# Roots of the layer norms on GpSimd, and the row maxima of attention split after one transpose

## The reference

```python
x = x + _L0_xattn_ref(_layernorm(x), ctx, ...)   # 8 heads of 8 channels, 256 positions, rotary
x = x + _L0_ffn_ref(_layernorm(x), ...)          # 64 experts, top 8, width 96
x = x + _L1_xattn_ref(_layernorm(x), ctx, ...)
x = x + _L1_ffn_ref(_layernorm(x), ...)

def _layernorm(x, axis=-1, eps=1e-05):
    m = jnp.mean(x, axis=axis, keepdims=True)
    v = jnp.var(x, axis=axis, keepdims=True)
    return (x - m) / jnp.sqrt(v + eps)
# in attention, per head:
scores = jnp.einsum('bhtc,bhsc->bhts', q, k) / math.sqrt(K_CH)
p_attn = jax.nn.softmax(scores, axis=-1)
```

## Time and profile before

| | us |
|---|---|
| median of 3 runs | 2429.53 (2429.11 to 2438.61) |
| the profiled execution | 2436.11 |
| its span in the profile | 2434.3 |
| busy in it: PE, DVE, ACT, POOL | 1719.1, 1632.6, 1215.9, 963.7 |

### The profile page before, as it was taken

The page is one execution under the profiler, slowest core; times in us unless marked ns, Lnnn a source line. Parts: engine busy times, 40 slices in busy tenths (PEclk is TensorE's granted clock), DMA queues, the critical chain, the costliest instruction groups (busy, mean ns, idle before and its releaser), DMA issues. The chain is left out here.

```text
span 2434.3 us, 45523 instructions
## 1 busy us (share of the span) xinstructions
PE 1719.1 (71%) x12720; PEld 1137.5 (47%) x12879; DVE 1632.6 (67%) x5762; ACT 1215.9 (50%) x3109; POOL 963.7 (40%) x878
## 2 busy tenths in 40 slices
PE   1488888888883688888888347777777777755651
PEld 0244444444441577777777214344444344434431
DVE  3588888888883334444432368999999999983331
ACT  0266666666671345555555226656556556642120
POOL 0115555555556000000000255555655656227883
PEclk9899999999996799999999759999999999988896
DMA  6855656565546875445454577665666656408856
GB/s 154 192 141 166 170 165 169 168 170 170 166 140 203 277 227 159 154 152 161 152 158 151 192 186 200 165 167 157 159 168 158 167 152 161 120 28 223 184 98 109
DMA packets 420687, 399.24 MB, mean 164 GB/s; under 512 B 46171, under 2 KB 392667, under 8 KB 420443
## 3 DMA queue, kind: packets, MB, share of 16 engines
q1 hardware_dynamic: 345163, 264.16, 39.2%
q0 software_dynamic: 37904, 90.22, 14.6%
q10 hardware_dynamic: 37376, 41.96, 5.9%
HBM read 242.00 MB, written 178.42 MB: 173 GB/s over the span
## 5 line engine op out<-in xcount | busy, mean ns | idle before, releaser
L786 ACT ACTIVATE prob<-psE 128x512 f32<-128x512 f32 x1024 | 600.0, 600 | 389.6 <-PE psE L1378 377.5
L987 DVE TENSOR_REDUCE mx<-psS 128x2 f32<-128x512 f32 x1024 | 682.9, 676 | 93.8 <-PE psS L1367 81.5
L674 POOL DMA_INDIRECT yg<-y_d,posb x256 | 263.3, 1029 | 880.6 <-DVE posb L1047 593.5
L1378 PE MATMUL psE<-q,k 128*128 128x256 bf16 x2048 | 397.9, 277 | 44.1 <-DMA q<-mrow 17.9
L1316 DVE TENSOR_TENSOR hid<-sil,psE 128x96 f32<-128x96 f32 x384 | 97.6, 254 | 429.1 <-ACT sil L872 428.7
L1367 PE MATMUL psS<-k,q 128*128 128x512 bf16 x865 | 339.5, 395 | 51.6 <-DMA k<-k_stack_d 31.4
L1483 PE MATMUL psE<-wt,xgT 128*128 (+1 forms) x1536 | 330.8, 340 | 0.3
L662 POOL DMA_INDIRECT xs_d<-xr,posi x256 | 250.6, 979 | 187.6 <-ACT prob L786 146.4
L1477 PE MATMUL psS<-ident,xg 128*128 128x128 f32 x768 | 158.4, 289 | 194.4 <-DMA xg<-xn_d,idx 83.1
L867 ACT COPY xgT<-psS 128x256 f32<-128x256 f32 x384 | 144.4, 376 | 288.8 <-PE psS L1477 254.7
L1378 PEld LDWEIGHTS psE<-q,k 128*128 128x128 bf16 x2048 | 194.2, 99 | 185.1 <-ACT prob L786 26.0
(11 more groups left out here) (209 smaller groups left out, 2842.5 us busy)
## 6 DMA issues: line engine op xcount, KB each, us to landing
xg<-xs_d SPq DMA_DIRECT2D x320, 128.0 KB, 2.1
y_d<-y_all SPq DMA_DIRECT2D x320, 128.0 KB, 1.8
q<-q_stack_d SPq DMA_DIRECT2D x128, 256.0 KB
k<-k_stack_d SPq DMA_DIRECT2D x128, 256.0 KB
wt<-in_gu ACTq DMA_DIRECT2D x128, 192.0 KB, 3.8
wt<-in_dn ACTq DMA_DIRECT2D x128, 96.0 KB, 4.2
q_stack_d<-parts SPq DMA_DIRECT2D x64, 192.0 KB
k_stack_d<-parts SPq DMA_DIRECT2D x64, 192.0 KB
```

What stands on the lines that cost most here:

```text
L674: g.indirect_dma_start(yg[:, k, :], None, y0_d[:, :], bass.IndirectOffsetOnAxis(posb[b][:, k:k + 1], 0)).then_inc(d_yg, 16)
L786: a.activation(prob[gr][:, u % 4, :], psE[ring][:, :], ACT.Exp, scale=SCALE).then_inc(s_exp, 1)
L987: v_.tensor_reduce(mx[b][:, bg // 4, :].rearrange("p (h r) -> p h r", h=2)[:, :, (bg % 4) * 2 + tt], psS[(UNITS * (st.s0 - LAG["smax"]) + ...
L1378: ins = m_.matmul(psE[ring][:, i * T:(i + 1) * T], k2[b][:, bg, hh * T + i * P:hh * T + (i + 1) * P], q2[b][:, bg, :], start=True, stop=True)
```

## The change

1. **Roots.** POOL computes them at the head of the step, ahead of its first indirect DMA: two operations on 128x2 (variance plus epsilon, negated mean), a power of -0.5, and a product, with a wait between those that depend on each other. The twelve DVE instructions go. ACT waits for the new count in unit 6, and DVE waits for it in unit 15, before it overwrites `mv`.
2. **Maxima.** The reduction writes negated maxima (`negate=True`). PE transposes 16 columns of f32 directly (`mT1` as before in unit 1, `mT0` in unit 10 instead of 11). ACT copies the transpose as bf16 (`mhi`; half 0 in unit 11 instead of 12), and DVE subtracts that from the transpose (`mlo`; half 1 in unit 3, half 0 in unit 12). SP sends `mhi` and `mlo`, one DMA each, after `mlo`. The bank is free only after `mlo`. L995, L1003 and L1004 go.
3. In layer 1 DVE's residual (L1132) moves from unit 10 to unit 9 and the comparison L1143 from 9 to 10.

```diff
+    def roots(self):
+        return self.s0 - LAG["front"] + 1 + self.L * (STEPS - LAG["front"] - 2)
...
-        FREE = dict(mT0=s_mrow[0], mT1=s_mrow[1], V=s_v, OT0=s_nrm[0], OT1=s_nrm[1], Q=s_qr, K=s_kr,
+        FREE = dict(mT0=s_mlo[0], mT1=s_mlo[1], V=s_v, OT0=s_nrm[0], OT1=s_nrm[1], Q=s_qr, K=s_kr,
...
-                    hold(sp, s_mrow[1], st.n("attn"))
-                    for hh in range(2):
-                        sp.dma_start(q2[b][64 * hh + MAXROW:64 * hh + MAXROW + 2, 4:8, :].rearrange("p g t -> p (g t)"),
-                                     mrow[1][16 * hh:16 * hh + 16, :]).then_inc(d_max[1][b], 16)
+                    hold(sp, s_mlo[1], st.n("attn"))
+                    for i, part in enumerate((mhi[1], mlo[1])):
+                        sp.dma_start(q2[b][MAXROW + i:MAXROW + i + 65:64, 4:8, :].rearrange("p g t -> p (g t)"),
+                                     part[:, :]).then_inc(d_max[1][b], 16)
...
+            g.memset(power[:, :], -0.5)
...
+                if st.on("front") or st.on("route"):
+                    if st.on("front"):
+                        pool.wait_ge(s_mvx, st.n("front"))
+                    if st.on("route"):
+                        pool.wait_ge(s_mvr, st.n("route"))
+                    done = 4 * (st.roots() - 1)
+                    wait(pool, s_rstd, done)
+                    g.tensor_scalar(ve[:, :], mv[:, :, 1], EPS, None, ALU.add).then_inc(s_rstd, 1)
+                    g.tensor_scalar(below[:, :], mv[:, :, 0], -1.0, None, ALU.mult).then_inc(s_rstd, 1)
+                    pool.wait_ge(s_rstd, done + 2)
+                    g.tensor_tensor(rstd[:, 0, :], ve[:, :], power[:, :], ALU.pow).then_inc(s_rstd, 1)
+                    pool.wait_ge(s_rstd, done + 3)
+                    g.tensor_tensor(rstd[:, 1, :], below[:, :], rstd[:, 0, :], ALU.mult).then_inc(s_rstd, 1)
                 moved(0, PACE[0])
...
-                    a.copy(mrow[h][:, :], psM[item_bank(L, f"mT{h}")][0:32, 0:P]).then_inc(s_mrow[h], 1)
+                    a.copy(mhi[h][:, :], psM[item_bank(L, f"mT{h}")][0:16, 0:P]).then_inc(s_mhi[h], 1)
...
-                    if u == 12 and st.on("smax"):
+                    if u == 11 and st.on("smax"):
                         max_rows("smax", 0)
                     if u == 6 and (st.on("front") or st.on("route")):
-                        act.wait_ge(s_rstd, st.it * 3 + (st.s0 - 1 + L * (STEPS - 4)))
+                        act.wait_ge(s_rstd, 4 * st.roots())
...
-                                     psS[...][:, :].rearrange("p (h s) -> p h s", h=2), AX.X, ALU.max)\
+                                     psS[...][:, :].rearrange("p (h s) -> p h s", h=2), AX.X, ALU.max, negate=True)\
...
-                def negate_max(h):
-                    ...
-                def split_max(h):
-                    ...
+                def split_max(stage, h):
+                    dve.wait_ge(s_mhi[h], st.n(stage))
+                    v_.tensor_tensor(mlo[h][:, :], psM[item_bank(L, f"mT{h}")][0:16, 0:P], mhi[h][:, :], ALU.subtract)\
+                      .then_inc(s_mlo[h], 1)
...
-                    if u <= 5 and norms:
-                        newton(2 * u)
...
-                    if u < 5 and norms:
-                        newton(2 * u + 1)
...
+                    if u == 3 and st.on("attn"):
+                        split_max("attn", 1)
+                    if u == 12 and st.on("smax"):
+                        split_max("smax", 0)
...
+                    if u == 15 and (st.on("front") or st.on("route")):
+                        dve.wait_ge(s_rstd, 4 * st.roots())
...
-                        product("mT1", "attn", [(s_msp[1], st.n("attn", 2))],
-                                [(msp[1][:, :, :, :].rearrange("p h a r -> p (h a r)"), None)], s_mT[1])
+                        product("mT1", "attn", [(s_max, st.n("attn", UNITS))],
+                                [(mx[st.buf("attn")][:, 1, :], None)], s_mT[1])
...
-                    if u == 11 and st.on("smax"):
-                        product("mT0", "smax", [(s_msp[0], st.n("smax", 2))],
-                                [(msp[0][:, :, :, :].rearrange("p h a r -> p (h a r)"), None)], s_mT[0])
+                    if u == 10 and st.on("smax"):
+                        product("mT0", "smax", [(s_max, st.n("smax", UNITS, 8))],
+                                [(mx[st.buf("smax")][:, 0, :], None)], s_mT[0])
```

More of the change, by code:

```diff
@@ L49 @@
 EPS = 1e-5
-MAGIC = 1597463007.0
 STRIDE = TOKENS
@@ L187, in build @@
         tok0 = sb("tok0", [P, 1])
+        power = sb("power", [P, 2])
         part_i = sb("part_i", [P, 1], I32)
@@ L240, in build @@
         mx = [ab(f"mx{b}", [P, 2, 16]) for b in range(NB)]
-        mhi = [ab(f"mhi{h}", [P, 2, 8], BF16) for h in range(2)]
-        msp = [ab(f"msp{h}", [P, 2, 2, 8]) for h in range(2)]
-        mrow = [ab(f"mrow{h}", [32, P], BF16) for h in range(2)]
+        mhi = [ab(f"mhi{h}", [16, P], BF16) for h in range(2)]
+        mlo = [ab(f"mlo{h}", [16, P], BF16) for h in range(2)]
         v = [ab(f"v{b}", [P, 2, UNITS, 32]) for b in range(NB)]
@@ L251, in build @@
         stats = ab("stats", [P, 2, 6])
-        nwt = ab("nwt", [P, 6, 2])
+        ve = ab("ve", [P, 2])
+        below = ab("below", [P, 2])
         rstd = ab("rstd", [P, 2, 2])
@@ L590, in body @@
                     b = st.buf("smax")
[L591 to L594, removed]
+                    hold(sp, s_mlo[0], st.n("smax"))
+                    for i, part in enumerate((mhi[0], mlo[0])):
+                        sp.dma_start(q2[b][MAXROW + i:MAXROW + i + 65:64, 0:4, :].rearrange("p g t -> p (g t)"),
+                                     part[:, :]).then_inc(d_max[0][b], 16)
                 if st.on("back"):
@@ L770, in max_rows @@
                     act.wait_ge(s_mT[h], st.n(stage))
-                    wait(act, d_max[h][(st.s0 - LAG[stage] - 1) % NB], Step(L, st.s0 - 1, st.it).nbuf(stage, 32)
-                         if st.s0 - 1 >= LAG[stage] else 0)
-                    a.copy(mrow[h][:, :], psM[item_bank(L, f"mT{h}")][0:32, 0:P]).then_inc(s_mrow[h], 1)
+                    before = Step(L, st.s0 - 1, st.it)
+                    if before.s0 >= LAG[stage]:
+                        act.wait_ge(d_max[h][before.buf(stage)], before.nbuf(stage, 32))
+                    a.copy(mhi[h][:, :], psM[item_bank(L, f"mT{h}")][0:16, 0:P]).then_inc(s_mhi[h], 1)
                 for u in range(UNITS):
@@ L1114, in body @@
                         normalise(1)
-                    if u < 5 and norms:
-                        newton(2 * u + 1)
-                    if u == 5 and norms:
-                        ch.join("newton")
-                        v_.scalar_tensor_tensor(rstd[:, 1, :], mv[:, :, 0], -1.0, rstd[:, 0, :], ALU.mult, ALU.mult)\
-                          .then_inc(s_rstd, 1)
                     if L == 0 and u == 8 and st.on("front"):
@@ L1124, in body @@
                         rotate(1)
-                    if u == 8 and st.on("smax"):
-                        negate_max(0)
-                    if L == 1 and u == 10 and st.on("back"):
+                    if L == 1 and u == 9 and st.on("back"):
                         b = st.buf("back")
@@ L1137, in body @@
                         v_.tensor_reduce(posf[b][:, :], hot[:, :, :], AX.X, ALU.add).then_inc(s_posf, 1)
-                    if u == 8 and st.on("smax"):
-                        split_max(0)
-                    if u == 9 and st.on("place") and L == 1:
+                    if u == 10 and st.on("place") and L == 1:
                         b = st.buf("place")
@@ L1179, in body @@
                             v_.tensor_copy(topf[b][:, :], topi[b][:, :]).then_inc(s_topf, 1)
-                    if u == 15 and st.on("smax"):
-                        negate_max(1)
                     if u == 14 and st.on("back"):
@@ L1196, in body @@
                         v_.bn_aggr(mv[:, 1, :], stats[:, 1, :]).then_inc(s_mvr, 1)
-                    if u == 15 and st.on("smax"):
-                        split_max(1)
                     if u == 15 and st.on("comb"):
```

38 lines of the change are left out of this document (2 added, 36 removed).

## The result

The changed kernel takes 2450.1 us (median, 2443.3 to 2455.1) beside 2430.2 us (2428.7 to 2438.6) for the kernel before on the same chip. The ratio is 1.0065, with a 95% interval of 1.005 to 1.008: slower by 0.65%, where 3.4% faster was forecast. Later runs of the changed kernel on another chip gave 1.004 (1.0028 to 1.0053).

A forecast was written before the change was run, and what follows sets the result against it. DVE was taken to bound layer 1, with DVE, PE and POOL taking turns in layer 0. Savings of 25 us (layer 0) and 57 us (layer 1), 82 together, took 2429.5 to 2348 us; own range 2325 to 2370, cost bounds 2312 to 2394.

The forecast's parts named there:

- rival (e): POOL's power is long: past 7.2 us in layer 0 ACT waits in unit 6; 2457 us at 8.9 us; chance 5%.
- V's bank: PSUM bank for PE's V product, freed by the unit 3 subtraction: PE waits later for the rotation anyway, so no cost.
- the blocking 0.5 us a step: Layer 1, DVE waiting for POOL: 0.5 of the Newton steps' 1.5 us of waiting stays; bounds 0 and 1.5.
- Rival (a): Layer 1's additions inherit the waiting for POOL; layer 1 saves 0.9 us a step, 27 us; 2378 us; chance 17%.
- Layer 1's term of 1.9 us: DVE in layer 1: 2.76 less 0.4 less 0.5 us saved a step, 57 us over thirty steps; bounds 27 and 75.
- Layer 0: 0.85 forecast: DVE between mask and rotation in layer 0: 0.85 us saved a step, 25 us over thirty steps; bounds 9 and 42.
- The nearer bound: Layer 0's low bound: 0.3 us a step (9 us), if PE takes DVE's place in its third of the loop.
- DVE's wait for the logits: Sign expected in layer 0: DVE's wait for the router's logits, 0.92 us before, grows to about 2 us.
- SP's queue: Half 1's rows and the loads behind them go about four and a half us later in layer 1; fits, counted 0.
- rival (b): The loads come late: layer 1's step stays at 22, layer 0 gains nothing; 32 us saved, 2398 us; chance 13%.
- POOL's four operations: POOL's new work on 128x2 each step: 1.5 us for the four with waits, between 0.6 and 4.7, covered by existing waits.
- rival (d): Negation in DVE's reduction costs 0.08 us each for 1024 reductions, 82 us, cancelling the gain; 2430 us; chance 4%.

The follow-up runs named there:

- third run: Changed kernel with half 1's subtraction in DVE's unit 1 instead of 3, both layers; ratio 0.9805 to the kernel before.
- the eleventh: Changed kernel, subtraction still in unit 3, with POOL's L704 and L705 of layer 1 behind the second gather, not the first; ratio 0.9913.
- eighth run: Kernel before with only the maxima's part, DVE keeping Newton, half 1 subtracted in unit 3 in layer 0 and unit 1 in layer 1; ratio 1.0049.
- sixth run: Changed kernel with subtraction in unit 3 in layer 0 and 1 in layer 1, plus layer 1's L704 and L705 ahead of POOL's first gather; ratio 0.977.

## Why the prediction was wrong

It forecast 2348 us, and even rival (e), the slow side, needed a power of 8 us. Step by step:

**V's bank: the step that failed.** The prediction says: "V's bank now comes free with the subtraction in unit 3 and no longer with ACT's copy in unit 1; by the same starts PE would come to V some 0.2 us early, and it waits later in the loop for the rotation anyway, so nothing." That was worked out from the rows of layer 0, and there it held: V's product waits for `mlo` once in 400 us, 0.5 us. It was never asked for layer 1, which has no rotation, and where PE stands further ahead of DVE. The trace of the kernel before shows it: V's product starts 2.9 us before DVE is through with its third addition, behind which the subtraction was to go.

```profile
1654.89 0.61 PE L1409 MATMUL psM<-proj_v,ctx 128*128 128x128 f32 x4
1657.31 0.47 DVE L1084 SCALAR_TENSOR_TENSOR x<-yg,w_all,x 128x256 f32<-128x256 f32 x1
```

Layer 1 had a later wait to hide it in, Q's for `nrm`, but of 1.6 us only. The subtraction's place was worth 2 to 2.5 us a step there: 24.16 and 24.33 with unit 3, 21.84 and 22.08 with units 2 and 1. That figure holds both what the subtraction sets free, V's bank and SP's queue; that the bank alone is enough is shown by 24.44 us with the loads early. The wait was named, but not who is queued behind it (the scores of the next units), nor what DVE does in front of the subtraction in the other layer.

**What stands ahead of the subtraction.** The prediction gave the blocking 0.5 us a step (the addition takes 1.33 us over) and asked only how much DVE work it adds. Its place mattered more: 1.6 to 1.8 us of the loss are the blocked addition right ahead of the subtraction that PE waits for (unit 3 with POOL's pair later, 22.56). The two unseen costs do not simply add: unit 3 without the blocking costs 0.7 us, and the blocking behind the subtraction costs V nothing.

**Rival (a), the additions inherit the waiting,** had the mechanism: the third addition takes 1.80 us. Its size for the whole change was 0.9 us a step in layer 1. With the subtraction in unit 2 or 1, so with V's bank out of the way, the change gives 1.4 and 1.2; the roots alone give 0.95, where its own terms leave 0.8 (2.29 less 1.5). Its time, 2378 us, did not come out either, as it too had V's bank at nothing. The argument against it was an order of starts, that the third addition would come ahead of POOL's operation. It does (1706.37 and 1706.71) and is blocked all the same. The Trainium skill, SBUF — State Buffer, section "Who interferes with whom", has that a DVE operation with two SBUF inputs contends with a GpSimd operation that reads SBUF, and one with at most one SBUF input, outside its two-port modes, does not. The trace agrees beside L704, for the additions (1.80) and `exm` (1.86), and for the subtraction with one input in PSUM (0.27). It does not agree beside L705, which reads SBUF too, with one tensor as input: the fourth addition lies within it in all 25 steps from 1500 to 2100 us and takes 0.46 us (1709.02 above). So the additions wait for L704 alone. A small operation can still lose time beside the other: in the kernel before, the Newton step L975 takes 0.43 us there, not 0.15.

**Layer 1's term of 1.9 us** had two further faults of size. DVE's busy time in the unit 2 kernel is 557.9 of 600 us, 20.3 a step, and before 569.9, 22.1: 1.8 us less, near the forecast. But its idle time rose from 1.2 to 1.5 us a step, and the step fell by 1.4. The forecast took all that leaves DVE for gain, as if 97% busy meant that no other wait would come.

**Layer 0: 0.85 forecast, 0.41 measured,** and 5.7 us from first to last, not 25. The nearer bound named it: "if PE takes the place of DVE in its third". DVE's third of the loop (MAX8 to rotation) shrank from 8.0 us (507.12 to 515.12) to 7.5 (500.68 to 508.18), with a new idle time of 0.42 us in it ahead of a reduction. Without that it would be 0.9 shorter. The waits for scores went from 1.5 to 3.0 us a step. The roots alone bring 0.29, the maxima alone nothing. DVE's wait for the logits didn't grow to 2 us as the prediction wanted; the time that left DVE went into its waits for PE.

**SP's queue: "it just fits, and I count 0".** It did not fit: 31.3 us of PE waits for `k_stack_d` ahead of the scores in 600, and 9.6 more ahead of the transposed ones. Loads less late than that, with the bank free, cost some 13 us; taking the lateness away with the bank still held brings little: 1.0025 (1.0005 to 1.0046) on one chip against 1.004 (1.0028 to 1.0053) and 1.0065 on others, 24.44 us a step. So rival (b) is true in kind and not needed for the loss. How it would compare in size at its full lateness stays open.

**POOL's four operations: nearly right.** Estimated at 1.5 us for the four with their waits; from the first start to the last end they take 1.6 us in layer 0 and 1.9 in layer 1 (means of 26 steps). The busy times alone are 253 + 224 + 818 + 209 = 1504 ns. Their cover held: the roots alone made the kernel faster. Rival (e) falls with the 0.82 us of the power.

**Negation: right.** The reductions went from 676 to 680 ns over the span; rival (d) would have had 755.

Not settled: what sets the 21.8 to 22.1 us of the good variants, where neither DVE (93%) nor PE is full and moving the blocking changed nothing; what the late loads alone would cost; and the uneven steps of layer 0, which show in the profiles of the third run (unit 1) and of the eleventh (unit 3).

## What to carry to other kernels

An edit that puts an operation later is to be costed once for every loop it is in: for each, who waits for it in order, what stands behind that waiter, and what stands in front of the moved operation on its own engine at its worst measured length, not its mean. A later wait of the same waiter can hide a new one, but only as much of it as that later wait lasts. A blocked operation is cheap where nobody waits for the next one and dear right ahead of a bank's release, so look at the neighbours before moving either. And a busy share of 97% says what to take away first, not that all that is taken away comes back.

## What the runs showed of the hardware

- DVE's third addition starts 0.34 us ahead of POOL's `hot` (1706.37 and 1706.71), where it alone would take 0.47 us, and still takes 1.80; in the kernel of the eighth run `exm` starts 0.45 us ahead (1703.08 and 1703.53), where it takes 0.22 elsewhere, and takes 1.86. POOL's gather, which ends right before, is what runs at that point. So the blocking here begins ahead of the recorded start of the operation that seems to cause it. In the kernel of the sixth run, with no gather between, one addition started 0.25 us ahead of `hot` (1937.12 and 1937.37) and took 0.48: it was not blocked.
- Of POOL's pair only `hot` (two tensors as input, 1.17 us) blocks DVE's additions; beside the one-tensor operation behind it (1.76 us) they take 0.46 us.
- A power on POOL takes 818 ns on 128x2, four times the 209 ns of a multiplication of that size; in the changed kernel it takes 0.72 us in layer 0 and 0.99 in layer 1.
- PE's clock fell to the 1.2 GHz level right after an idle time of 3 us (1.00 in 1707 to 1708 without work, 0.71 and 0.50 in the two after), so this wait of PE cost more than its length: V's product took 1.19 us against 0.61. Over 1450 to 2050 us the mean granted clock is 0.92 in the changed kernel, 0.98 before and with unit 2.
- The negate flag of a reduction over 128x512 cost about 4 ns (676 and 680); with unit 2 the reduction with the flag takes 674.
